# Attention with 64-row score tiles, log-weights added by TensorE, and denominators normalised through DMA

## The reference

```python
# 16 heads of 16 features, S = 256
Q, K, V = proj(Wq, bq), proj(Wk, bk), proj(Wv, bv)
lam = 10 * exp(-5 * u_prev)                      # one number a batch
use_sparse = lam >= 1
scores = einsum('bhqd,bhkd->bhqk', Q, K) * 0.25
dense  = softmax(scores + lam * where(prior_mask, 0, -1)) @ V
sparse = softmax over 32 gathered keys (idx[q, j], some may repeat) @ V[idx]
out = where(use_sparse, sparse, dense)
x = x + out @ Wo.T + bo
```

## Time and profile before

| what | value |
|---|---|
| median of 3 runs | 2219.41 us (2218.94 to 2220.04) |
| span of the profiled execution | 2220.5 us |
| attention in it | 0 to about 937 us |
| TensorE busy | 2051.3 us, 92% |
| VectorE busy | 1699.0 us, 77% |
| ScalarE busy | 1196.2 us, 54% |
| GpSimd busy | 796.4 us, 36% |

### The profile page before, as it was taken

One profiled execution on the slowest core, in us unless ns is written; L12 is line 12 of the kernel. 1 busy time (PEld: TensorE's weight loads), 2 busy tenths in 40 slices (PEclk: granted clock), 3 DMA queues, 4 the chain that ended last, 5 costly groups with the idle time before them and its releaser, 6 DMA issues. The chain is left out here.

```text
span 2220.5 us, 42789 instructions
## 1 busy us (share of the span) xinstructions
PE 2051.3 (92%) x14158; PEld 1652.1 (74%) x14158; DVE 1699.0 (77%) x2530; ACT 1196.2 (54%) x2428; POOL 796.4 (36%) x589
## 2 busy tenths in 40 slices
PE   3899999999999999759999999999995999999998
PEld 2566666666666666447777777777774999999997
DVE  6788888888888888577878888887875566666664
ACT  2466565666665666435555555555554555555553
POOL 4645444444455554033333333333340111111111
PEclk8999999999999999879999999999997999999998
DMA  3444444444444444100000000000001222222221
GB/s 92 106 106 107 107 110 110 108 109 108 105 105 106 108 109 104 24 25 1 0 0 0 0 0 0 0 0 0 0 0 59 78 79 70 85 69 80 85 66 60
DMA packets 121171, 137.47 MB, mean 62 GB/s; under 512 B 24240, under 2 KB 89776, under 8 KB 121136
## 3 DMA queue, kind: packets, MB, share of 16 engines
q1 hardware_dynamic: 118576, 128.64, 22.9%
q0 software_dynamic: 2560, 8.39, 1.0%
HBM read 48.35 MB, written 8.39 MB: 26 GB/s over the span
## 5 line engine op out<-in xcount | busy, mean ns | idle before, releaser
L366 DVE TENSOR_REDUCE a_neg_max<-a_s 128x2 f32<-128x512 f32 x512 | 329.1, 683 | 123.4 <-PE a_s L613 121.8
L487 ACT ACTIVATE a_e<-a_t 128x512 f32<-128x512 f32 x512 | 281.2, 610 | 228.4 <-PE a_t L626 228.4
L375 DVE SCALAR_TENSOR_TENSOR a_e<-a_e,a_w_t 128x1024 f32<-128x1024 f32 x256 | 373.6, 1469 | 4.1 <-ACT a_e L487 4.1
L613 PE MATMUL a_s<-a_k_st,a_q_st 96*128 96x256 f32 x1024 | 275.4, 380 | 0.0
L613 PEld LDWEIGHTS a_s<-a_k_st,a_q_st 96*128 96x128 f32 x1024 | 203.5, 199 | 13.7
L610 PE MATMUL a_s<-a_add_m,ident_bf 128*128 128x512 bf16 x512 | 201.8, 394 | 7.9 <-POOL a_add_m L254 5.8
L1695 ACT ACTIVATE c_hid<-c_pH,c_b 128x256 f32<-128x256 f32 x256 | 107.4, 471 | 186.3 <-PE c_pH L1758 185.9
L897 POOL TENSOR_TENSOR b_decayed<-b_table,b_mod_t 128x1024 f32<-128x1024 f32 x64 | 118.6, 1872 | 210.3 <-ACT b_mod_t L1163 203.0
L1317 PE MATMUL b_pS<-b_gated_t,b_decayed 128*128 128x256 f32 x768 | 189.5, 390 | 0.7
L626 PE MATMUL a_t<-a_q_st,a_k_st 97*128 97x512 f32 x512 | 177.1, 426 | 2.6 <-DMA a_q_st<-a_max_row 2.0
L642 PE MATMUL a_v<-a_e,a_v_pad 128*32 128x256 f32 x2048 | 163.6, 392 | 4.5 <-DVE a_e L375 2.1
(11 more groups left out here) (261 smaller groups left out, 5720.4 us busy)
## 6 DMA issues: line engine op xcount, KB each, us to landing
a_q_st<-a_q_hi SPq DMA_DIRECT2D x256, 128.0 KB, 2.4
a_k_st<-a_k_hi SPq DMA_DIRECT2D x256, 64.0 KB, 2.0
a_q_st<-a_q_lo SPq DMA_DIRECT2D x128, 128.0 KB, 2.4
a_xs<-in_xT SPq DMA_DIRECT2D x32, 256.0 KB, 2.8
a_k_st<-a_k_lo SPq DMA_DIRECT2D x128, 64.0 KB, 2.1
x_all<-in_xT SPq DMA_DIRECT2D x32, 256.0 KB, 2.8
c_we<-in_we SPq DMA_DIRECT2D x32, 256.0 KB, 2.7
c_key_t<-in_keyT SPq DMA_DIRECT2D x32, 256.0 KB, 3.2
```

Source lines behind the costliest of these rows:

```text
L366: dve.tensor_reduce(neg_max[:, qc, head:head + 2], ps_s[b][:], AX.X, ALU.max, negate=True).then_inc(red_done, 1)
L375: dve.scalar_tensor_tensor(out=buf[:], in0=buf[:], scalar=BIG, in1=w_t[par][:, kc].unsqueeze(1).to_broadcast([P, 4, S]), op0=ALU.min, op1= ...
L487: act.activation(e[g % E_BUFS][:, 2 * b:2 * b + 2], ps_t[b][:], ACT.Exp).then_inc(exp_done, 1)
L613: ins = pe.matmul(ps_s[b][:, r], q_st[par][0:96, slot, qc * P:qc * P + P], k_st[par][0:96, slot // 2], start=False, stop=(r == 1))
```

## The change

- Heads are placed so that 64 partitions hold the stack of one half of the heads: three products of 16 rows, 48 rows, with the maximum as a 49th. Partitions 0 to 63 and 64 to 127 are two row tiles (`tile_position=(64 * r, 0)`), each with its own bank. `members(g)` replaces `rows_group(g)`.
- `score_rows` has no mask matmul; VectorE adds the mask while it takes the maximum (`tensor_tensor_reduce`, four of 256 columns a group).
- The weights enter as logarithms: `score_cols` adds `log_w`, in a high and a low part, by four 512-column matmuls against the identity; then come four tiled matmuls of 256 columns. `weigh` is gone. The order of `body` on TensorE has `score_cols` ahead of the projections.
- The denominators go through DRAM: POOL sends them from the raw values to `den_rows`, back as `den` on 128 partitions, VectorE takes reciprocals, POOL sends them to `r_rows` and back, repeated, as `r_rep`. Four DMAs from ACT's queue (`merge`) bring the two halves of the raw values together. `collect`, `spread` by matmul, `combine` and the copy `even` are gone.
- Q is projected without the two masked copies; high and low parts of Q and K are made by one instruction each; the stacking DMAs stay 24 a batch, each of 64 KB.
- The first block with its constants is gone. The counts are made by 64 independent compares in bf16 on VectorE that TensorE adds up; then the logarithm is taken on ACT.

```diff
         def stack(n, par, half):
             sp.wait_ge(stack_free[half], n + 1)
-            for done, dst, src, terms in ((khi_done, k_st[par], k_hi, (0, 1)), (qhi_done, q_st[par], q_hi, (0, 2)),
-                                          (klo_done, k_st[par], k_lo, (2,)), (qlo_done, q_st[par], q_lo, (1,))):
+            for done, term, first, step in ((hi_done, 0, 1, 1), (lo_done, 1, 1, 2), (lo_done, 2, 0, 2)):
                 sp.wait_ge(done, n + 1)
...
+                for r in range(2):
                     for j in (2 * half, 2 * half + 1):
...
         def maxima(n, par):
             sp.wait_ge(mrow_done, n + 1)
-            sp.dma_start(q_st[par][96:97].bitcast(F32), max_row[:].bitcast(F32)).then_inc(d_max, 16)
+            for r in range(2):
+                sp.dma_start(st[par][64 * r + 48:64 * r + 49, 0].bitcast(F32), max_row[8 * r:8 * r + 8].bitcast(F32))\
+                  .then_inc(d_max, 16)
...
+        def denominators(n):                                  # POOL
+            at_least(pool, d_den, n * 16)
+            for half in range(2):
+                pool.wait_ge(raw_done, 2 * n + half + 1)
+                pool.dma_start(den_rows[:, half], raw_v[half][16 * (1 - half)::32].rearrange("j c s -> j (c s)")).then_inc(d_row, 16)
+            pool.wait_ge(d_row, 32 * (n + 1))
+            pool.dma_start(den[:], den_rows.rearrange("j h (m k) -> (j h m) k", k=32)).then_inc(d_den, 16)
+        def spread(n):
+            pool.wait_ge(rden_done, n + 1)
+            pool.dma_start(r_rows.rearrange("j h (m k) -> (j h m) k", k=32), rden[:]).then_inc(d_r, 16)
+            pool.wait_ge(d_r, 16 * (n + 1))
+            pool.dma_start(r_rep[:]..., r_rows... repeated to 16 partitions a row).then_inc(d_rep, 16)
         def body(n, par, proj, maxi, finish):
+            if finish:
+                denominators(n - 1)
             if proj:
                 masks(n + 2, par)
+            if finish:
+                spread(n - 1)
             if maxi:
-                weights(n + 1, 1 - par)
+                sparse_weights(n + 1)
             if proj:
                 low_parts(n + 2)
...
         def row_max(n, par, g):                               # VectorE
-            for b in range(2):
-                dve.wait_ge(s_done, 2 * (n * GROUPS + g) + b + 1)
-                dve.tensor_reduce(neg_max[:, qc, head:head + 2], ps_s[b][:], AX.X, ALU.max, negate=True).then_inc(red_done, 1)
+            dve.wait_ge(s_done, n * GROUPS + g + 1)
+            for r in range(2):
+                for c in range(C):
+                    dve.tensor_tensor_reduce(out=ps_s[r][:, c], in0=ps_s[r][:, c], in1=add_m[par][:, qc], scale=1.0, scalar=-BIG,
+                                             op0=ALU.add, op1=ALU.max, accum_out=top[:, qc, head:head + 1]).then_inc(red_done, 1)
...
                 if g == 2 and finish:
                     reciprocal(n - 1)
-                if g == 4 and finish:
+                if g == 4 and maxi:
+                    log_weights(n + 1, 1 - par)
+                if g == 5 and finish:
                     normalize(n - 1)
...
+        def merge(n):                                         # ACT, at g == 1
+            act.wait_ge(d_row, 32 * (n + 1))
+            act.wait_ge(raw_done, 2 * (n + 1))
+            for j in range(4):
+                act.dma_start(raw_v[0][32 * j + 16:32 * j + 32], raw_v[1][32 * j + 16:32 * j + 32]).then_inc(d_merge, 16)
...
         def score_rows(n, par, g):                            # TensorE
-            for b in range(2):
-                pe.wait_ge(red_done, 2 * (n * GROUPS + g) + b - 1)
-                pe.matmul(ps_s[b][:], ident_bf[:], add_m[par][:, qc]..., start=True, stop=False)
-                for r in range(2):
-                    ins = pe.matmul(ps_s[b][:, r], q_st[par][0:96, slot, ...], k_st[par][0:96, slot // 2], ...)
+            pe.wait_ge(red_done, 4 * (n * GROUPS + g))
+            for c in range(C):
+                for r in range(2):
+                    rows = slice(64 * r, 64 * r + 48)
+                    ins = pe.matmul(ps_s[r][:, c], st[par][rows, 0, j, c, qc * P:qc * P + P], st[par][rows, 1, j, c],
+                                    start=True, stop=True, tile_position=(64 * r, 0))
         def score_cols(n, par, g):
             if g == 0:
-                pe.wait_ge(d_max, 16 * (n + 1))
+                pe.wait_ge(d_max, 32 * (n + 1))
+                pe.wait_ge(w_ready, n + 1)
-            for b in range(2):
-                pe.wait_ge(exp_done, 2 * (n * GROUPS + g) + b - 1)
-                pe.matmul(ps_t[b][:], k_st[par][0:97, ...], q_st[par][0:97, ...], start=True, stop=True).then_inc(t_done, 1)
+            pe.wait_ge(exp_done, 2 * (n * GROUPS + g))
+            for part in range(2):
+                for r in range(2):
+                    pe.matmul(ps_t[r][:], ident_r[:], log_w[par][:, part, kc].unsqueeze(1).to_broadcast([P, C, S]),
+                              start=(part == 0), stop=False)
+            for c in range(C):
+                for r in range(2):
+                    rows = slice(64 * r, 64 * r + 49)
+                    ins = pe.matmul(ps_t[r][:, c], st[par][rows, 1, j, c, kc * P:kc * P + P], st[par][rows, 0, j, c],
+                                    start=False, stop=(c == C - 1), tile_position=(64 * r, 0))
...
             for g in range(GROUPS):
                 if maxi:
                     score_rows(n + 1, 1 - par, g)
+                score_cols(n, par, g)
                 if g == 0 and proj:
                     project_q(n + 2, par)
                 if g == 1 and proj:
                     project_k(n + 2, par)
-                score_cols(n, par, g)
-                if finish:
-                    if g == 2:
-                        collect(n - 1)
-                    elif g == 3:
-                        spread(n - 1)
-                    elif g == 7:
-                        project_out(n - 1)
+                if g == 7 and finish:
+                    project_out(n - 1)
```

More of the change, by code:

```diff
@@ L32, in at_least @@
     eng.wait_ge(sem, value)
-def rows_group(g):
-    half, c, rows = g // 4, g // 2 % 2, g % 2
-    return 2 * c + half, rows
 def landed(n, par):
@@ L277, in residual @@
+        def low_parts(n):
+            pool.wait_ge(hi_done, n + 1)
+            if not (isinstance(n, int) and n == 0):
+                for half in d_stack:
+                    pool.wait_ge(half, n * 16 * STACK_DMAS)
+            pool.tensor_tensor(split[:, 0::3], full[:], split[:, 1:3].bitcast(F32), ALU.subtract).then_inc(lo_done, 1)
         def residual(n):
@@ L298, in _ @@
         low_parts(1)
-        weights(0, 0)
+        sparse_weights(0)
         masks(1, 1)
         batches(pool, body)
+        denominators(NB - 1)
+        spread(NB - 1)
         residual(NB - 1)
@@ L387, in reciprocal @@
[L387 to L395 removed]
+                dve.wait_ge(m_ready, n + 1)
+            dve.wait_ge(s_done, n * GROUPS + g + 1)
+            dve.sem_inc(scores_seen, 1)
@@ L617, in score_cols, with count @@
-        def score_cols(n, par, g):
-            quad, kc = rows_group(g)
-            if g == 0:
-                pe.wait_ge(d_max, 16 * (n + 1))
-            for b in range(2):
-                if not (isinstance(n, int) and n == 0 and g == 0):
-                    pe.wait_ge(exp_done, 2 * (n * GROUPS + g) + b - 1)
-                pair = 2 * quad + b
-                pe.matmul(ps_t[b][:], k_st[par][0:97, pair, kc * P:kc * P + P],
-                          q_st[par][0:97, 2 * pair:2 * pair + 2], start=True, stop=True).then_inc(t_done, 1)
+        def count(k):
+            for j in range(K_SPARSE):
+                pe.wait_ge(hot_done, k * K_SPARSE + j + 1)
+                pe.matmul(ps_v[0][:, k], ident_bf[:], hot[:, j], start=(j == 0), stop=(j == K_SPARSE - 1)).then_inc(hot_mm, 1)
@@ L716, in body @@
             mix_values(n, par, GROUPS - 1)
-        pe.wait_ge(scaled, 4)
-        for n in range(2):
-            project_q(n, n)
-            project_k(n, n)
-            if n == 0:
-                project_v(0, 0, 0)
-                project_v(0, 0, 1)
+        pe.wait_ge(d_const, 16 * len(CONSTS))
+        pe.wait_ge(d_w, 16 * 4)
+        pe.wait_ge(d_b, 16 * 4)
+        for m in range(C):
+            for k in range(C):
+                ins = pe.matmul(ps_t[1][:, 0, m:m + 1], wo[:, k, m * P:m * P + P], bias[:, 2, k:k + 1],
+                                start=(k == 0), stop=(k == C - 1))
+        ins.then_inc(setup_mm, 1)
+        pe.wait_ge(scaled, 2)
+        project_q(0, 0)
+        project_k(0, 0)
+        pe.wait_ge(const_cast, 2)
+        count(0)
+        project_v(0, 0, 0)
+        project_v(0, 0, 1)
+        count(1)
+        pe.wait_ge(const_cast, 3)
+        project_q(1, 1)
+        project_k(1, 1)
         turn_counts()
@@ L729, in _ @@
         batches(pe, body)
-        collect(NB - 1)
-        spread(NB - 1)
         project_out(NB - 1)
@@ L1897, in column, with slots @@
         return b.reshape(-1, P).T
```

(5 more changed lines are left out.)

470 lines of the change are left out of this document (198 added, 272 removed).

## The result

The changed kernel takes 2449.44 us (median of 4 runs, 2446.08 to 2451.68), the kernel before beside it 2219.72: a ratio of 1.1031 (95% interval 1.1016 to 1.1047), 229.7 us slower. The forecast was 2380, with a range of 2275 to 2490: the direction and the engine that sets the pace were right, the size was 70 us short, and most of that stands in a term that the forecast had left out, the granted clock.

A forecast was written before the change was run, and what follows sets the result against it. TensorE was taken to bound the kernel. A batch of 32.2 us, 5.15 more, gave +155 over 30 batches; with +13 at the end and 0 at the start, 2220 became 2388, forecast as 2380 us, range 2275 to 2490.

The forecast's parts named there:

- Plain group 2.84: TensorE's attention loop: a group takes 2.84 us against 2.07 before; bounds 1.99 and 3.3.
- rival 1: Row tiles run one after the other: 0.48 us a group more, period 36, 2500 us; chance 0.10.
- rivals 3 and 4: Rival 3: a switch costs 0.1 only, 2280, chance 0.11; rival 4: switches free, loads hidden, 2195 to 2205, chance 0.05.
- Projections unchanged at 7.2: TensorE's rest of a batch (Q, K, V and output projections, transposes) stays at 7.2 us.
- Wait for the maxima 1.6: TensorE idles 1.6 us a batch before the first identity matmul, until the maxima's two DMAs land.
- Rival 2: The clock falls at the new gap: half of 6.8 us lost every batch, +102, 2480 us; chance 0.10.
- three signs of being wrong: Group near 2.1 us, VectorE waiting for DRAM transfers, or the clock low inside the loop.
- 0.62: Upper bound in us for one VectorE add-and-max instruction, if it has an accumulator read; lower bound 0.42, taken 0.55.
- DRAM road hidden: POOL's four serial transfers of denominators and reciprocals, and the low parts, all hidden with 2 to 3 us to spare.
- rival 5: A DRAM transfer takes 5.5 us, so a batch waits 1 to 2 us in VectorE: about 2425; chance 0.04.
- End +13: Last batch: unfilled groups take 24.4 us against 18.9, and the four transfers add 8; together +13 us.
- Start 0: Start of attention: shorter count steps offset the logarithm and slower first row-score groups; 0 us, bounds -10 and +15.

The follow-up runs named there:

- e_serial: Changed kernel with both tiled score matmuls of row tile 0 issued first, then those of row tile 1, in place of alternating: 2453.66 us, ratio 1.1041.
- e_tilefirst: Changed kernel with the 64-row score matmuls of the column scores ahead of the identity matmuls: 2400.32 us, ratio 1.0808.
- e_fill: Changed kernel with seven unused 512-column matmuls filling TensorE's gap before each batch's first identity matmul: 2406.08 us, ratio 1.0828.
- b_dram: Kernel before with only the denominators' road through DRAM and the DMA merge of value halves, replacing collect, spread, combine and copies: 2240.81 us, ratio 1.0088.
- b_dram2: Kernel before with the DRAM road and DMA merge, POOL's mask in one step, and column scores of groups 0 and 1 ahead of Q and K projections: 2276.8 us.
- e_nodram: Changed kernel without the four DRAM transfers of denominators and reciprocals and without the reciprocal, so no division by the softmax sum: 2398.57 us, ratio 1.0807.
- e_logw: Changed kernel with VectorE's log-weight instructions moved from behind the maxima of group 4 to behind those of group 7: 2416.23 us, ratio 1.0879.

## Why the prediction was right, and where its size was off

- *What bounds it:* TensorE, right. Taking work off VectorE gained nothing.
- *Plain group 2.84:* measured 2.81. The parts: rows 0.43 (0.45), identity 1.13 (1.20), tiled 0.43 (0.52), values 0.57 (0.67); the difference is the wait for exp, which I had put beside the group. The assumed overlap of row tiles holds (e_serial's starts), so rival 1 is out; a change of shape costs 0.2, so rivals 3 and 4 are out.
- *Projections unchanged at 7.2:* mis-sized, they take 8.2. Q and K had whole-array matmuls on both sides and took 1.54; now they have tiled ones on both and take 1.92 (1.82 in e_tilefirst, where only those behind are tiled). The V parts and the output projection had tiled values behind them before, and grew by 0.1 each.
- *Wait for the maxima 1.6:* 2.05. *Exp 0.6:* 0.5. *ACT's merge 0.3:* no row shows it. The sum of 32.2 meets the 31.9 of the batches at full clock, and that is in part luck: the groups' own work was put 2.2 too high (22.7 against 20.5), the projections 1.0 and the waits 0.9 too low (VectorE's 0.65 was not among them).
- *Rival 2, the clock:* this is the term that failed: the sum had it at nothing, and of my own three signs of being wrong one came, the low clock inside the loop. I gave it a chance of 0.10 as an alternative, with 3.4 us lost in every batch. It is real and less than half that size: 3.4 us at half clock in most batches, 1.6 lost each time, 41 us by e_fill. The last batch of before had shown it, and I counted it away because more idle time followed there. That caution had something in it, since in e_tilefirst the same wait passes without a fall; the fault was to leave the term out of the sum.
- *VectorE:* four add-and-max instructions take 1.53 us a group and not 2.2; 0.38 from start to start lies below my lower bound of 0.42. The accumulator read of the Trainium skill ("VectorE: DVE Perf Modes", Two Vector instructions with no wait between them) does show as an instruction of its own, 142 ns; but it runs beside the next one, so the 0.62 did not apply.
- *DRAM road hidden:* right for the output, wrong for POOL's queue. With 5.5 us for r_rep, rival 5's time of a transfer came true for that one (the others take 1.7 to 2.1), not its path: normalize does not wait, but the sparse weights, the log weights and group 5 do (0.65 a batch).
- *End +13:* 20. From the last transposes to the end of the last values it is 31.7 us against 21.9, 10 more where I had 5.5: groups of 2.86 at full clock are near the 3.05, but three ran at half clock. The four transfers cost 7.1 more (13.5 against 6.4; forecast 8), and what follows them 3. *Start 0:* +5.5; VectorE waited 13.6 us for the logarithm, and the row-score groups stood 2.7 apart.

In the error of 62 us against the worked sum of 2388 the loop has 46 (41 of clock by e_fill, 7 of the late batch, and 2 less for the rest), the end 7, the start 5.5, the later layers 2.5, for which no run gives a cause.

## What to carry to other kernels

Ask which engine paces the kernel before paying with its time: here VectorE had 13% to spare and TensorE 1%. A wait of 2 us on the pacing TensorE costs its own length and can cost half clock behind it (in 24 of 31 batches of the changed kernel, in 8 of e_tilefirst); if the profile shows that anywhere, book it as a term of the sum, with a lower bound of nothing, and not as a rival. And a queue that waits for a transfer holds up everything behind it, so follow each wait to the last instruction of its queue, and look at what that instruction then runs beside.

## What the runs showed of the hardware

- Each change between tiled and whole-array matmuls costs about 0.2 us: 0.1 in which the last matmuls end, and 0.1 of a load that nothing covers. The Trainium skill ("TensorEngine Tiling (Array Packing)", Key Properties) says that changing the mode drains TensorE; the traces agree and give the price.
- Two row tiles overlap, whether their matmuls are issued in turn or one tile behind the other: pairs start 3 to 7 ns apart in both kernels, and the time differs by 4 us of 2450 (e_serial).
- A stretch of 2.0 us in which TensorE is idle, once a batch, was followed by 3.4 us at 1.2 GHz in most batches of the changed kernel and in few of e_tilefirst; with the stretch filled it was not (e_fill).
- VectorE's weighing reads two operands from SBUF and takes 1.21 us alone. Where a tensor-tensor instruction of POOL held it up, it ended 1.08 to 1.10 us behind the end of that instruction: it did next to nothing beside it. That gives 2.04 us where 0.96 of the instruction were left and the 2.81 of b_dram. In b_dram2 the second subtraction is recorded as starting before the first has ended, and the weighing waited through both: 4.84. The Trainium skill ("SBUF — State Buffer", Who interferes with whom) says that a VectorE instruction with two inputs in SBUF contends with a POOL instruction that reads SBUF, and that the shared ports are an exclusive lock; the traces agree for POOL's tensor-tensor.
- Which of the two comes first is not read from the starts alone. In the kernel before, 44 weighings started ahead of POOL's tensor-tensor and all kept their 1.21 us, and so did 42 in b_dram. In b_dram and b_dram2 one weighing a batch started 0.15 to 0.41 us ahead of it, while POOL was still issuing a DMA, and was held up all the same. Why, no run here shows.
- The log weights have two operands in SBUF too: 2.76 us beside POOL's subtraction in the changed kernel, 0.75 in e_nodram and e_logw, where they no longer meet it.
